# Scoring two heads together in separate row groups of TensorE, instead of one head at a time over zero-padded keys

## The reference

```python
q = (x @ wq).reshape(Bq, Tq, N_KV, N_REP, HEAD_DIM)          # 2 groups of 4 heads
k_lat = (x @ wk_down).reshape(Bq, Tq, N_KV, D_LAT)           # 32 latents a group
k = jnp.einsum('bkhl,ld->bkhd', k_lat, wk_up)
scores = jnp.einsum('bqhrd,bkhd->bhrqk', q, k) * scale
scores = jnp.where(causal, scores, jnp.finfo(scores.dtype).min)
probs = jax.nn.softmax(scores, axis=-1)
```

## Time and profile before

| | us |
|---|---|
| median of 3 runs | 1282.39 |
| lowest, highest | 1281.73, 1282.71 |
| the profiled execution, its own time | 1286.94 |
| its span in the trace | 1285.2 |
| mean granted clock of TensorE | 0.917 of 2.4 GHz |

### The profile page before, as it was taken

How to read it: one execution, slowest core, us unless ns; L and a number is a source line. 1 busy time by engine, 2 the same in 40 slices (tenths; PEclk the granted TensorE clock), 3 DMA queues, 4 the chain that set the end, 5 groups by cost and what they waited for, 6 DMA issues and landing times. The chain is left out here.

```text
span 1285.2 us, 19659 instructions
## 1 busy us (share of the span) xinstructions
PE 1032.5 (80%) x6224; PEld 698.6 (54%) x6224; DVE 995.8 (77%) x2205; ACT 749.6 (58%) x1483; POOL 649.0 (50%) x470
## 2 busy tenths in 40 slices
PE   5895679888997889878988889978998888877191
PEld 4552136565655566555655565655665565655191
DVE  3766988689788988899888988798878977698301
ACT  2544346477647766586648775676647764575030
POOL 0103952189335962298236953297326942198402
PEclk9896569999999999999999999999988998989596
DMA  5202202262144513271145414270235404171441
GB/s 168 75 9 66 75 2 94 77 222 82 32 155 149 164 30 128 56 253 50 32 155 181 140 32 148 61 243 30 66 115 182 139 23 146 37 244 44 162 163 42
DMA packets 74152, 137.24 MB, mean 107 GB/s; under 512 B 10505, under 2 KB 44345, under 8 KB 73921
## 3 DMA queue, kind: packets, MB, share of 16 engines
q1 hardware_dynamic: 67936, 123.20, 29.3%
q0 software_dynamic: 5392, 12.59, 3.2%
q10 hardware_dynamic: 720, 0.19, 0.1%
HBM read 116.34 MB, written 15.42 MB: 103 GB/s over the span
## 5 line engine op out<-in xcount | busy, mean ns | idle before, releaser
L1709 DVE TENSOR_TENSOR_SCAN probs_T<-bank,probs_T 128x512 f32<-128x512 f32 x256 | 301.2, 1212 | 3.6 <-POOL probs_T L599 2.6
L601 POOL TENSOR_TENSOR probs_T<-step_space,probs_T 128x1024 f32<-128x1024 f32 x112 | 263.5, 2359 | 0.0
L1265 ACT ACTIVATE bank<-step_space,a_neg 128x512 f32<-128x512 f32 x256 | 169.7, 685 | 81.5 <-DVE probs_T L1709 78.6
L1190 ACT ACTIVATE probs<-bank,row_neg 128x128 f32<-128x128 f32 (+3 forms) x256 | 134.9, 529 | 125.0 <-DVE row_neg L1570 108.5
L896 PE MATMUL bank<-k_pad,q_lat 128*128 128x512 f32 (+3 forms) x512 | 186.1, 450 | 3.4 <-DMA k_pad<-xc 3.4
L1570 DVE TENSOR_REDUCE row_neg<-bank 128x1 f32<-128x128 f32 (+3 forms) x256 | 122.6, 486 | 79.9 <-PE bank L898 77.7
L1369 DVE TENSOR_TENSOR probs<-probs_T,bank 128x1024 f32<-128x1024 f32 x128 | 153.6, 1200 | 11.1 <-POOL step_space L630 11.0
L633 POOL TENSOR_TENSOR step_space<-step_space,probs 128x512 f32<-128x512 f32 x112 | 142.5, 1273 | 36.9 <-DVE probs L1369 35.8
L860 PE MATMUL bank<-probs,w_ident 128*128 128x512 f32 x256 | 153.1, 683 | 8.4 <-DVE probs L1369 8.4
L571 POOL DMA_INDIRECT slots_dram<-xn_slots,slot x64 | 62.7, 979 | 154.3 <-issue 154.3
L807 PE MATMUL bank<-expert_w,hidden 128*128 128x128 f32 x960 | 139.8, 292 | 0.0
(11 more groups left out here) (214 smaller groups left out, 1816.8 us busy)
## 6 DMA issues: line engine op xcount, KB each, us to landing
expert_w<-in_experts_dram SPq DMA_DIRECT2D x120, 512.0 KB, 5.1
probs_T<-b_rows_dram SPq DMA_DIRECT2D x64, 512.0 KB, 4.5
slots_in<-slots_dram SPq DMA_DIRECT2D x24, 256.0 KB, 3.4
results_dram<-slots_out SPq DMA_DIRECT2D x24, 256.0 KB, 4.1
k_pad<-xc SPq DMA_DIRECT2D x64, 64.0 KB, 2.0
x_in<-in_x_dram POOLq DMA_DIRECT2D x8, 256.0 KB, 3.3
gate<-gate_rows_dram SPq DMA_DIRECT2D x1, 2048.0 KB, 7.1
out_dram<-x_out POOLq DMA_DIRECT2D x7, 256.0 KB, 3.6
```

The costliest lines, as they stand in the source:

```text
L601: ins = nc.gpsimd.tensor_tensor(inject[:, n % 3, :, :], u[:], row.unsqueeze(1).to_broadcast([P, DH, T]), ALU.mult)
L1190: f(probs_ring[:, n % 4, 0:(i + 1) * P], bank[SCORE_BANK[n % 4]][:, 0:(i + 1) * P], ACT.Exp, bias=row_neg[:, n % 4:n % 4 + 1], accum_out=r ...
L1265: f(decay(k)[:], delta[:, c, :], ACT.Exp, scale=a_neg[:, c, n:n + 1]).then_inc(dec_ok.sem, 1)
L1709: v.tensor_tensor_scan(state[:, n % 2, c, :], decay(DH * n + c)[:], inject[:, n % 3, c, :], 0.0, ALU.mult, ALU.add).then_inc(st_ok.sem, 1)
```

## The change

Two heads are scored together, head j of a pair out of rows 32 j to 32 j + 31 of the array, each over its own 32 partitions of `q_lat` and `keys`, into two banks; the two mask matmuls follow. So `k_pad`, its memset, the 8 DMAs a batch and all waits for them are gone. `keys` is a tile of its own and no longer shares the space of `xc`. PE waits for the copy `k_lat` itself. `scores` is called for even n only and makes the units n and n+1; it now waits for the exponential of unit n-3, whose bank unit n+1 takes. `last_sum` stands at n = 2, ahead of the pair (2, 3), because unit 3 writes bank 1.

```diff
-        k_pad = sb("k_pad", [P, G, HG, T])
+        keys = sb("keys", [P, G, T])
...
-            def place_keys(b):
...
-                        sp.dma_start(k_pad[j * L:(j + 1) * L, g, j, :], k_four[j * L:(j + 1) * L, g, :]
-                                     ).then_inc(k_out.sem, 16)
...
                 def scores(n):
                     g, i, j = n // (NT * HG), n // HG % NT, n % HG
                     if n == 0:
-                        pe.wait_ge(k_out.sem, k_out.at(b, 16 * G * HG))
+                        pe.wait_ge(k_lat.sem, k_lat.at(b, G))
...
                     if n >= 4:
-                        pe.wait_ge(s_exp.sem, s_exp.at(b, n - 3))
-                    s = bank[SCORE_BANK[n % 4]]
-                    mm(s[:, 0:(i + 1) * P], q_lat[:, g, i * P:(i + 1) * P], k_pad[:, g, j, 0:(i + 1) * P],
-                       start=True, stop=False)
-                    mm(s[:, i * P:(i + 1) * P], ident_bf[:], mask_bf[:], start=False, stop=True).then_inc(s_mm.sem, 1)
+                        pe.wait_ge(s_exp.sem, s_exp.at(b, n - 2))
+                    for h in range(j, j + 2):
+                        head = slice(h * L, (h + 1) * L)
+                        mm(bank[SCORE_BANK[h % 4]][:, 0:(i + 1) * P], q_lat[head, g, i * P:(i + 1) * P],
+                           keys[head, g, 0:(i + 1) * P], start=True, stop=False)
+                    for h in range(j, j + 2):
+                        mm(bank[SCORE_BANK[h % 4]][:, i * P:(i + 1) * P], ident_bf[:], mask_bf[:], start=False, stop=True
+                           ).then_inc(s_mm.sem, 1)
...
-                    if n < UNITS:
+                    if n < UNITS and n % 2 == 0:
                         scores(n)
...
-                if ahead:
-                    act.wait_ge(k_out.sem, k_out.at(b + 1, 16 * G * HG))
                 take_conv(0)
...
-            v.memset(k_pad[:], 0.0).then_inc(pad_zero, 1)
...
-LAST_SUM, LAST_READ, PE_MIXER, DVE_MIXER, TAKE_X, NORM_UNIT = 3, 2, 6, (3, 7), 8, 8
+LAST_SUM, LAST_READ, PE_MIXER, DVE_MIXER, TAKE_X, NORM_UNIT = 2, 2, 6, (3, 7), 8, 8
```

More of the change, by code:

```diff
@@ L211, in build @@
         xc = sb("xc", [P, DH, T])
-        k_four = xc
         res_gate = sb("res_gate", [P, DH, T])
@@ L244, in build @@
         weights_in = sem("weights_in")
-        pad_zero = sem("pad_zero")
         first_in = sem("first_in")
@@ L282, in build @@
         k_lat = signal("k_lat", G)
-        k_out = signal("k_out", 16 * G * HG)
         v_mm = signal("v_mm", 1)
@@ L429, in _ @@
         def _(sp):
-            def place_keys(b):
-                for g in range(G):
-                    sp.wait_ge(k_lat.sem, k_lat.at(b, g + 1))
-                    if g == 0:
-                        sp.wait_ge(pad_zero, 1)
-                    for j in range(HG):
-                        sp.dma_start(k_pad[j * L:(j + 1) * L, g, j, :], k_four[j * L:(j + 1) * L, g, :]
-                                     ).then_inc(k_out.sem, 16)
             for name in first_a:
@@ L520, in start_experts @@
                 fetch_slots(b)
-            place_keys(1)
             spread_rows(0, False)
@@ L525, in _ @@
                 start_experts(b - 1)
-                place_keys(b + 1)
                 spread_rows(b, True)
@@ L1139, in take_keys @@
                 act.wait_ge(q_mm.sem, q_mm.at(b, G + g + 1))
-                f(k_four[:, g, :], bank[PRE_BANK][:], ACT.Copy).then_inc(k_lat.sem, 1)
+                f(keys[:, g, :], bank[PRE_BANK][:], ACT.Copy).then_inc(k_lat.sem, 1)
             def take_values(b):
@@ L1281, in _ @@
                 act.wait_ge(q_mm.sem, q_mm.at(0, g + 1))
-                f(k_four[:, g, :], bank[FIRST_BANK[g]][:], ACT.Copy).then_inc(k_lat.sem, 1)
+                f(keys[:, g, :], bank[FIRST_BANK[g]][:], ACT.Copy).then_inc(k_lat.sem, 1)
             for g in range(G):
```

1 line of the change is left out of this document (removed).

## The result

The changed kernel took 1308.6 us, the median of four runs from 1300.8 to 1314.8, against 1282.6 us for the kernel before beside it. The ratio is 1.0186, with a 95% interval from 1.0133 to 1.0239. The forecast was 1280.4 us, in a range from 1271 to 1294: wrong in sign and outside the range. Of the rivals, the third came true, to which I had given 0.06: TensorE's clock falls in the attention.

What follows compares the result with a forecast made beforehand. PE was taken to bound batch 0; in batch 4, taken as typical, PE and DVE are both full and DVE's chain sets the end. 1282.4 - 2.5 - 3 + 3.5 = 1280.4 us, range 1271 to 1294.

Steps and rivals of the forecast that it cites:

- What a pair costs: Scores on TensorE: full overlap, 0.30 us of switching a pair; 1.17 us instead of 1.74 at 512 columns.
- The start: Batch 0's first exponential: first pair no longer waits for the DMAs that place the keys, -2.5 us.
- The stages, +0.5 each: Attention stages of batches 1 to 7: each 0.5 us longer, seven stages +3.5 us.
- (d): Rest of the stage: DVE's chain, late by 0.5 us from the mixer's end, sets the end; PE's gain is spent waiting.
- (a): First pair of a stage: 0.52 us where the first score took 0.22, so maxima and product come later, +0.25 us.
- (c): Unit 7's score no longer behind the mixer's output matmul: of 0.75 us some 0.5 stay, as units 8 and 9 come together.
- (b): Last sum, now followed by the pair (2, 3): +0.5 us, and the whole end of the mixer with it.
- Batch 0, -3: Batch 0 behind its first exponential, PE the bound, partly at 1.2 GHz: pairs save 3 us, between -1 and -9.
- rival 1: Cheap switches (-2 instead of +3.5) or batch 0's clock recovers (-9 instead of -3): 1274 to 1275 us, both 1269; chance 0.18.
- rival 3: TensorE's clock falls in the attention through more holes: 2 to 4 us a stage, 1295 to 1309 us; chance 0.06.

Runs made afterwards that it cites:

- e4_fill1_11: The changed kernel with two thrown-away float32 matmuls of 512 columns on 128 rows a stage, behind units 1 and 11: 1288.8 us.
- e8_pairs_512: The kernel before, padded keys and DMAs kept, with only the eight units of 512 columns in pairs over their own rows: 1275.1 us.
- e11_pairs_fill: e8_pairs_512 with one thrown-away matmul behind the next batch's projections: 1271.5 us.
- e7_before_fill: The kernel before with the two thrown-away matmuls of e4_fill1_11: 1289.5 us.
- e2_padded: The changed kernel with its pairs and waits, but zero-padded keys on all 128 rows and their DMAs instead of row groups: 1297.2 us.
- e3_fill11: The changed kernel with one thrown-away float32 matmul of 512 columns on 128 rows behind unit 11: 1296.1 us.
- e13_384_full: The kernel before with units of 512 and 384 columns in pairs, and one thrown-away 512-column matmul on 128 rows behind unit 11: 1278.7 us.
- e5_rows32: e4_fill1_11 with its two thrown-away matmuls over 32 rows instead of 128: 1307.4 us.
- e15_f11_rows32: e3_fill11 with its one thrown-away matmul over 32 rows instead of 128: 1300.4 us.
- e16_f11_half: e3_fill11 with its thrown-away matmul cut to 256 columns, on 128 rows: 1294.1 us.
- e1_single: The changed kernel with each head issued alone over its 32 rows, in the order and with the waits of the kernel before: 1502.5 us.

## Why the prediction was wrong

**What a pair costs: right.** Overlap in full, and 0.30 us of switching. I had put it at 0.15 in and 0.15 out; it is 0.09 in front, 0.10 between the passes and 0.10 behind. The Trainium skill, "TensorE: Matmul & The Clock Gate", Part 3, has 3.07 times for four row groups of 512 columns; half of it, 1.54, was my estimate for a pair, and I called it a case between full and no overlap. Here two heads' passes, 4 x 0.43 = 1.71 us of columns, took 1.06 us to the masks, or 1.6 times, and that is full overlap with 0.2 us of switches in it. The trace is near that estimate; no run here has four row groups together.

**The start: right,** -3.1 us for -2.5. The 0.5 us more come from the table load, which starts at 22.12 and not at 22.60.

**The stages, +0.5 each: wrong in sign, at full clock, by term (d).** From a stage's first score to its end the changed kernel with its extra matmuls takes 40.4 to 40.7 us in batches 2, 4, 5 and 6 of e4_fill1_11, against 40.8 before. Terms (a) to (c) came nearly as worked out. In batch 4 of the changed kernel the first score starts at 618.28, the product 1.10 us behind it (before 1.02), the mixer's sum 4.51 (before 3.94) and x_mid 9.51 (before 9.76):

```profile
618.28 0.49 PE L881 MATMUL bank<-keys,q_lat 32*128 32x128 f32 x4
...
619.38 1.21 DVE L1353 TENSOR_TENSOR probs<-probs_T,bank 128x1024 f32<-128x1024 f32 x1
...
622.80 0.74 DVE L1519 SCALAR_TENSOR_TENSOR step_space<-xc,w_d_skip,bank 128x512 f32<-128x512 f32 x1
...
627.79 0.69 DVE L1526 TENSOR_TENSOR x_mid<-x,bank 128x512 f32<-128x512 f32 x1 [0.81 <-PE bank L859]
```

So (a) was 0.1 for 0.25, (b) 0.5 as forecast, and x_mid 0.25 us earlier where I had 0.13. The maximum of unit 8 comes 0.32 us later, for 0.26. The mistake is (d): it took the mixer's end for late by 0.5, against (c), and let DVE's chain take up all that PE gains behind it. The units of 512 columns did gain: in e8_pairs_512 units 12 to 15 take 4.67 us instead of 5.05 and units 28 to 31 3.35 instead of 3.62, the latter in the changed kernel as well. So a stage is 0.1 to 0.4 us shorter and not 0.5 longer, some 4 to 6 us in all in the changed kernel's favour. This is not why the forecast failed.

**Batch 0, -3: off.** It gained 0.7 us in its stage and lost 2.6 between its stage and the first scan. It was thought out by the mean clock of before, and the clock fell further: 27.3 us of its stage at 1.2 GHz instead of 17.1. At like clocks the pairs do give what the term said, 3.9 us (e11_pairs_fill against e7_before_fill). Of rival 1 nothing came: the hole before the first score went, and the clock of batch 0 fell all the same.

**The clock: the step that failed.** The sum priced all of TensorE's freed time as harmless or useful, at the clock of the kernel before. I met the question in rival 3 and put it aside with one row: waits of 1.1 to 1.2 us in batch 4 leave 2.4 GHz in place. This was true of a kernel in which everything around these waits is 128 rows deep. The changed kernel has a longer wait (1.46), less work around it and a part of that work on 32 rows, and I compared only the length of a single wait. The rival's size, 14 to 28 us, holds the 26 us that came. Its distribution does not: not 2 to 4 us a stage but 1.5 in most, 7.7 more than before in batch 1, and 4.1 outside the stages. What the clock cost can only be estimated. Among the four executions of the changed kernel, 1300.8 us go with a mean clock of 0.894 and 1314.8 with 0.875: 14 us for some 53 us more at 1.2 GHz, 0.27 us for each. The profiled execution had 62 us more than that of before, which makes some 17 us; without them its span would be some 1282 us, near the forecast 1283.2, partly by errors that cancel. By the mean clocks of all four executions (0.885) and of the kernel before (0.925) it is some 108 us more, or 29 us, and the forecast was off by 28.

**Shown** is that the row groups and not the order lose the clock (e2_padded), that a useless matmul in the wait gives it back (e3_fill11, e4_fill1_11, e13_384_full), that it does nothing for a kernel that has not lost it (e7_before_fill), and, from few stages of one execution each, that rows count beside time (e5_rows32 against e4_fill1_11, e15_f11_rows32 against e16_f11_half). **Open** is why the stretches change their places between executions and behind each mended hole, what share of the loss between the stages belongs to the pairs, and what e1_single loses to its many 0.10 us pieces and what to its rows.

## What to carry to other kernels

Time that a change frees on TensorE is not neutral: ask of each stage whether what is left still holds the clock, counting the rows in use as well as the time, before pricing anything at 2.4 GHz. Row groups pay where the columns are many, since each visit to them costs 0.30 us whatever the width, and where TensorE would otherwise end the wait. Try part of a change: a quarter of the units in pairs gave 7.9 us, half of them cost 5 by the medians (9 by the ratio), and all of them, with the DMAs gone as well, 26.

## What the runs showed of the hardware

- Two float32 matmuls over different groups of 32 rows, issued one behind the other, overlap pass by pass: 1.06 us for 512 columns each.
- Entering and leaving the row groups costs 0.30 us a visit at 2.4 GHz, the same for one head as for two, and a third of it lies between the two passes of a float32 matmul. A head alone over 32 rows is so 0.3 us dearer than over 128 (0.94 us at 384 columns where two full passes have 0.64).
- The clock fell behind 13 us in which TensorE was busy throughout, and stayed low with it busy 10 of 10 us (e1_single). It fell at 3.02 of 3.40 us (e15_f11_rows32), and held at 2.39 of 3.40 with the extra matmul on full rows (e16_f11_half).
- With one thrown-away matmul of 0.43 us a stage at full rows the changed kernel took 1294.1 us instead of 1308.6 and 1310.2, by the ratios (1.0076 against 1.0186 and 1.0199) some 14 us less.
